# Context and token transfers issued first, and VectorE in place of ScalarE for the turned exponentials of three attentions

## The chip, the cores and the metric

The kernel runs on one core of one Trainium2 chip. The metric is the device time of one launch in microseconds (us), the median of several runs. Engines are written as the profile writes them: PE is TensorE (PEld its weight loads), ACT is ScalarE, DVE is VectorE, POOL is GpSimd, SP is SyncE, which here only issues transfers.

## What is computed

Four blocks run one after the other on x (16 x 128 tokens, 256 channels) with a context ctx of the same shape, all in fp32:

```python
x = _L0_xattn_ref(ctx, x, ...)   # 16 heads of 16: tokens attend to context and tokens (256 keys); MLP with gelu
x = _L1_xattn_ref(x, ctx, ...)   # 32 query heads on 8 key heads of 8: attend to the context (128 keys); layer norm
x = _L2_xattn_ref(x, ctx, ...)   # recurrent block: token shift, low-rank mixes, decays, scan over 128 tokens, channel mix
x = _L3_xattn_ref(x, ctx, ...)   # 16 heads of 16: attend to the normalised context (128 keys); gated residual
```

The three attentions (of blocks 0, 1 and 3) are softmax(q k + mask) v.

## The kernel before

The 16 sequences are worked off in eight pairs. The work on a pair is cut into four parts, entry (transposes of x and ctx, q, k and v of block 0, k and v of block 1), front (blocks 0 and 1), back (block 2 and the queries of block 3) and final (attention 3 and the output). The parts of neighbouring pairs are interleaved in phases: `start` has the entry of pair 0, `first` the front of pair 0 and the entry of pair 1, `second` front, back and entry of three steps, five `steady` passes have all four parts, and `closing`, `last` and `end` run the pipeline empty. `last` holds the back of the last pair and attention 3 of the pair before; `end` holds attention 3 of the last pair alone.

**The order of work is written out by hand.** Four texts, PE_ORDER, ACT_ORDER, DVE_ORDER and POOL_ORDER, list the steps of each engine in the order in which it runs them, `@` giving the phase. Every engine works its list off in order, and each step waits on counting semaphores for what it needs. So what stands in front of a step on its own engine sets when it can begin.

An attention job n is a chain of five steps. `scores` (PE, L719, four jobs at a time into the four banks psS), `mask` (DVE, L1213: mask and negated maximum, into one of four buffers S), `exps` (ACT, L1029: exponentials and their sum, into one of two buffers E), `turn` (PE, L730: four 128x128 transposes into one of three ring banks of PSUM) followed by the copy of that bank into one of four buffers ET, and `weigh` (PE, L764 or L772: product with the values into psO). Attentions 0 and 1 have 16 jobs for a pair, attention 3 has 8. Which engine copies the turned exponentials is fixed by the table EMPTIES: ACT (L1016) for attentions 0 and 3, DVE (L1229) for attention 1. Every other product of PE goes through the same three ring banks, and a bank is written again only when the product three places earlier in PE's list has been copied out.

Names that come up later: `xT`, `cT` transposes of tokens and context; `q0`, `k0l`, `k0c`, `v0c`, `v0l`, `k1`, `v1` the entry's products; `aT` the normalised context; `norm`/`apply` the layer norms (DVE, with a root on POOL); `sum` the product with the inverse sums; `o1` the output of attention 1; `xaT`, `shift1`, `t` the head of block 2 (transpose L669, token shift, low-rank product L887); `vr0` to `vr7` its scans (DVE L1425, L1432), each followed by a product on POOL (L1569); `bonus` (L1412) and `g2` (L1407) two more steps of it on DVE; `yT`, `ynT` its group norm (L935, L669).

Before the lists there is a setup. SP issues W0 (q, k and v weights of block 0 in one transfer), the column constants colt, all seven bias rows rowt and the one-number gate, all on the semaphore s_w, and then context, tokens and mask of pair 0 and the other weights. PE, ACT, DVE and POOL each wait for all four transfers on s_w (64), and PE and POOL for DVE's constants too, before their first step:

```python
            sp.dma_start(W0t[:, 0:qkv], wl0[:, 0:qkv]).then_inc(s_w, 16)
            ...
            pe.wait_ge(s_setup_d, 4)
            pe.wait_ge(s_w, WEIGHTS_IN)
```

## Time and profile before

| | |
|---|---|
| median of three runs | 1126.52 us (1123.29 to 1128.92) |
| the profiled execution, its own time | 1128.1 us |
| its span | 1126.1 us |
| PE busy | 980.3 us, 87% |
| DVE busy | 806.4 us, 72% |
| ACT busy | 739.1 us, 66% |
| POOL busy | 256.7 us, 23% |
| mean granted clock of PE | 0.955 |

A busy share is an average over stages with different limits, so the kernel is read stage by stage. A row of the trace gives the start of a piece and its length, the engine and the line, and in brackets how long the engine had been idle before it and what ended that. The time of an execution is some 2 us more than its span.

### The profile page before, as it was taken

To read this page: it belongs to the slowest core of one execution; us is meant where nothing else is said; L and a number is where in the kernel's file an instruction comes from. 1 tells how busy PE (TensorE), PEld (TensorE's weight loads), DVE (VectorE), ACT (ScalarE), POOL (GpSimd) and SP (SyncE) were. 2 spreads that over 40 slices of the span, in tenths; PEclk is the share of its full clock that TensorE was granted. 3 is DMA by queue.
4 is the path that set the end of the run, shared out by engine and by line. 5 is a ranking of instruction groups with operands and counts; after the bars stand their busy time and mean duration, and the time that the engine had idled before them with its cause. 6 is when DMAs were issued, how large, how long until landed. Compare 5 with 4: busy or idle time off the path is not lost.

```text
span 1126.1 us, 23973 instructions
## 1 busy us (share of the span) xinstructions
PE 980.3 (87%) x7776; PEld 699.8 (62%) x7776; DVE 806.4 (72%) x3113; ACT 739.1 (66%) x2675; POOL 256.7 (23%) x349
## 2 busy tenths in 40 slices
PE   5779898998999899998999899998999899888356
PEld 4456566765766577665767577665766577556144
DVE  3408758886878776977878777987878776966623
ACT  1828853887658973788658983887658973881116
POOL 3102304031320413032321413031311413120300
PEclk9889999999999999999999999999999999989576
DMA  9100000000010000000010001000010000000000
GB/s 303 41 1 17 6 1 24 2 8 2 2 33 8 2 2 20 16 8 1 2 33 8 2 2 28 7 8 2 1 33 8 2 2 10 2 3 10 0 1 10
DMA packets 18091, 18.90 MB, mean 17 GB/s; under 512 B 7216, under 2 KB 16432, under 8 KB 17712
## 3 DMA queue, kind: packets, MB, share of 16 engines
q1 hardware_dynamic: 17968, 17.37, 5.1%
q8 instruction: 64, 1.05, 0.4%
q14 instruction: 59, 0.48, 0.1%
HBM read 15.27 MB, written 2.10 MB: 15 GB/s over the span
## 4 chain that ended last, share of the span: by engine, by line
PE 60%; DVE 14%; ACT 10%; issue 6%; POOL 2%; POOLq 0%; DVEq 0%; ACTq 0%
PE ring L678 16%; PE ring L688 15%; PE ring L730 9%; PE psS L719 5%; ACT E L1029 5%; DVE S L1213 3%; PE psO L764 2%; PE psO L772 2%; PE ring L897 2%; PE ring L669 2%; PE psO L805 2%; PE ring L887 1%; DVE slot L1389 1%; PE psS L788 1%; DVE SS L1432 1%
## 5 line engine op out<-in xcount | busy, mean ns | idle before, releaser
L1029 ACT ACTIVATE E<-S,nmax 128x128 f32<-128x128 f32 (+1 forms) x1024 | 423.7, 419 | 32.4 <-PE ring L730 21.3
L1213 DVE CUSTOM_DVE_ANT_0 S<-psS,mb 128x128 f32<-128x128 f32 (+1 forms) x1024 | 263.0, 319 | 39.8 <-ACT E L1029 17.2
L678 PE MATMUL ring<-slot,w_l 128*128 128x256 f32 x992 | 243.9, 393 | 16.5 <-ACT slot L990 12.3
L730 PE MATMUL ring<-ident,E 128*128 128x128 f32 x1280 | 202.3, 289 | 29.5 <-ACT E L1029 25.3
L678 PEld LDWEIGHTS ring<-slot,w_l 128*128 128x128 f32 x992 | 185.5, 195 | 54.8 <-ACT slot L990 14.6
L730 PEld LDWEIGHTS ring<-ident,E 128*128 128x128 f32 x1280 | 144.9, 145 | 101.8 <-ACT E L1029 63.0
L1029 ACT ACTIVATION_READ_ACCUMULATOR E<-S,nmax 128x1 f32 x1024 | 195.6, 191 | 0.0
L688 PE MATMUL ring<-w_l,slot 128*128 128x256 f32 (+1 forms) x640 | 155.1, 387 | 12.1 <-DVE slot L1453 4.7
L688 PEld LDWEIGHTS ring<-w_l,slot 128*128 128x128 f32 x640 | 116.3, 196 | 42.5 <-issue 8.8
L1016 ACT ACTIVATE ET<-ring 128x512 f32<-128x512 f32 x192 | 106.9, 587 | 17.2 <-PE ring L730 17.1
L719 PE MATMUL psS<-keys,slot 32*128 32x512 f32 (+1 forms) x768 | 97.3, 580 | 21.4 <-ACT ET L1016 12.8
L1432 DVE TENSOR_TENSOR_SCAN SS<-wP,kv 128x258 f32<-128x258 f32 x128 | 98.3, 809 | 9.7 <-POOL Z L1569 7.7
L990 ACT ACTIVATE slot<-ring 128x512 f32<-128x512 f32 x72 | 42.6, 594 | 81.1 <-PE ring L669 56.5
L1229 DVE COPY ET<-ring 128x512 f32<-128x512 f32 x128 | 84.1, 685 | 16.1 <-PE ring L730 16.1
L669 PE MATMUL ring<-ident,slot 128*128 128x128 f32 x384 | 62.9, 292 | 32.6 <-DMA slot<-in_x 12.8
L1213 DVE DVE_READ_ACCUMULATOR2_ANT nmax<- 128x1 f32 x1024 | 85.3, 83 | 0.0
L1569 POOL TENSOR_TENSOR Z<-SS,slot 128x512 f32<-128x512 f32 x64 | 77.1, 1204 | 35.7 <-DVE SS L1432 19.0
L1541 POOL TENSOR_TENSOR keys<-k0T,in 128x512 f32<-128x512 f32 x32 | 33.1, 1044 | 219.1 <-PE psS L719 212.7
L669 PEld LDWEIGHTS ring<-ident,slot 128*128 128x128 f32 x384 | 44.2, 146 | 55.5 <-issue 19.5
L1117 ACT ACTIVATE slot<-ring 128x512 f32<-128x512 f32 x8 | 4.8, 598 | 101.0 <-PE ring L935 101.0
L764 PE MATMUL psO<-ET,V 128*32 128x128 f32 x1536 | 64.8, 291 | 4.0 <-ACT ET L1016 3.3
L719 PEld LDWEIGHTS psS<-keys,slot 32*128 32x128 f32 x768 | 34.5, 187 | 38.6 <-ACT ET L1016 14.1
(120 smaller groups left out, 1131.7 us busy)
## 6 DMA issues: line engine op xcount, KB each, us to landing
slot<-in_ctx SPq DMA_DIRECT2D x8, 256.0 KB, 2.8
slot<-in_x SPq DMA_DIRECT2D x8, 256.0 KB, 2.8
w_l<-in_wl SPq DMA_DIRECT2D x1, 2048.0 KB, 10.7
out<-slot SPq DMA_DIRECT2D x8, 256.0 KB, 2.1
w_l<-in_wl SPq DMA_DIRECT2D x2, 768.0 KB, 6.6
w_l<-in_wl SPq DMA_DIRECT2D x1, 1152.0 KB, 8.5
m0i<-in_m SPq DMA_DIRECT2D x8, 128.0 KB, 3.1
mb<-in_m SPq DMA_DIRECT2D x8, 128.0 KB, 2.5
```

The costliest lines, as they stand in the source:

```text
L669: m = pe.transpose(b[:, c, a * P:(a + 1) * P], src[:, a, c * P:(c + 1) * P], ident[:, :])
L678: m = pe.matmul(b[:, a, :], w[:, k, m0 + a * P:m0 + (a + 1) * P], src[:, k, :], start=(k == 0), stop=(k == kt - 1))
L688: m = pe.matmul(b[:, bb, 0:n], src[:, k, bb * P:(bb + 1) * P], w[:, k, :], start=(k == 0), stop=(k == kt - 1))
L719: ins = pe.matmul(psS[m % QUAD][:, x * w:(x + 1) * w], queries, keys[rows, group % RING_K, x * w:(x + 1) * w], start=True, stop=True)
L730: m = pe.transpose(b[:, k, :], E[:, g % RING_E, k * P:(k + 1) * P], ident[:, :])
L764: m = pe.matmul(psO[32 * c:32 * c + 32, t, bb * P:(bb + 1) * P], v[:, window(8 * t + 4 * half + c, half, 16)], e, start=(half == 0 and sbl ...
L1016: act.activation(ET[:, g % 4, :, :], bank(phase, i, turned).rearrange("p a (h s) -> p (a h) s", h=2), ACT.Copy).then_inc(sems["emptied_A"], 1)
L1029: ins = act.activation(E[:, g % RING_E, h * w:(h + 1) * w], S[:, g % RING_S, h * w:(h + 1) * w], ACT.Exp, bias=nmax[:, g % 4, h:h + 1], sc ...
L1213: ins = dve.tensor_tensor_reduce(S[:, g % RING_S, h * w:(h + 1) * w], psS[g % QUAD][:, h * w:(h + 1) * w], bias[:, bb, :], -1.0, HUGE, ALU ...
L1229: dve.tensor_copy(ET[:, g % 4, :, :], bank(phase, i, turned).rearrange("p a (h s) -> p (a h) s", h=2))\
L1432: ins = dve.tensor_tensor_scan(SS[:, u % 2, a, :, :].rearrange("p b t -> p (b t)"), wP[:, ct, :, :].rearrange("p b t -> p (b t)"), kv[:, u ...
L1569: pool.tensor_tensor(Z[:, v % RING_Z, :, :].rearrange("p a (b t) -> p a b t", b=PAIR), SS[:, v % 2, :, :, 0:P], r, ALU.mult).then_inc(sems ...
```

## The change

1. SP issues context, tokens and mask of pair 0 first. The q, k and v weights of block 0 come as three transfers with a semaphore each, the two value-bias rows (128 partitions each) on their own, then W1, the gate and, after a wait for the v weights, the other five rows. Only colt still counts on s_w.
2. PE waits at the start for the identity only, and then at each product for its own weights. ACT and DVE wait for colt. POOL waits for the two head masks. DVE builds its other constants later, at its step `cols`, and the spread matrix is one copy of 256 columns in place of eight. The gate's tanh moves behind `aT`.
3. The table TURNED gives three attentions' turned exponentials to DVE: attention 0 of pair 0 (16 copies, phase `first`), attention 3 in `last` (8) and in `end` (8).
4. The four order texts are written anew, from `start` to `end`. Waits for score and output banks are found from the list of stages; they ask for the same events as before.

```diff
+TURNED = {("first", 0): "D", ("end", 3): "D", ("last", 3): "D"}
+def emptier(phase, name):
+    engines = TURNED.get((phase, name[1])) if name[0] == "turn" else None
+    return engines[name[2] % len(engines)] if engines else EMPTIES[name]
...
-            sp.dma_start(W0t[:, 0:qkv], wl0[:, 0:qkv]).then_inc(s_w, 16)
-            sp.dma_start(colt[:, :, :], cols).then_inc(s_w, 16)
-            sp.dma_start(rowt[:, :, :], rows.partition_broadcast(P)).then_inc(s_w, 16)
-            sp.dma_start(gate_t[:, 0:1], gate.partition_broadcast(P)).then_inc(s_w, 16)
...
             program("start", None)
+            sp.dma_start(W0t[:, 0:CT * C], wl0[:, 0:CT * C]).then_inc(s_wq, 16)
+            sp.dma_start(W0t[:, CT * C:2 * CT * C], wl0[:, CT * C:2 * CT * C]).then_inc(s_wk, 16)
+            sp.dma_start(colt[:, :, :], cols).then_inc(s_w, 16)
+            sp.dma_start(W0t[:, 2 * CT * C:qkv], wl0[:, 2 * CT * C:qkv]).then_inc(s_wv, 16)
+            for n in (ROWS.index("v0_b"), ROWS.index("v1_b")):
+                sp.dma_start(rowt[:, n:n + 1, :], rows[:, n:n + 1, :].partition_broadcast(P)).then_inc(s_row, 16)
             sp.dma_start(W1t[:, :], wl1).then_inc(s_w1, 16)
+            sp.dma_start(gate_t[:, 0:1], gate.partition_broadcast(P)).then_inc(s_gate, 16)
+            sp.wait_ge(s_wv, 16)
+            sp.dma_start(rowt[:, 1:len(ROWS) - 1, :], rows[:, 1:len(ROWS) - 1, :].partition_broadcast(P)).then_inc(s_rows, 16)
...
-            pe.wait_ge(s_setup_d, 4)
-            pe.wait_ge(s_w, WEIGHTS_IN)
+            pe.wait_ge(s_const, 2)
...
-            act.wait_ge(s_w, WEIGHTS_IN)
             act.wait_ge(s_const, 3)
-            act.activation(gate_t[:, 1:2], gate_t[:, 0:1], ACT.Tanh).then_inc(s_setup, 1)
+            act.wait_ge(s_w, 16)
...
-                    elif step[0] == "turn" and EMPTIES[step] == "D":
+                    elif step[0] == "turn" and emptier(phase, step) == "D":
                         copy_turned(*step[1:])
...
-            pool.wait_ge(s_w, WEIGHTS_IN)
-            pool.wait_ge(s_setup_d, 4)
+            ins.then_inc(s_zeros, 1)
+            pool.wait_ge(s_in32, 1)
```

Of the rewritten lists, three places show what moves.

ACT, from its first instruction (L984, before, is the gate's tanh; L990 and L1025 the copy of xT; L1001 and L1036 the keys; L1016 the copies of turned exponentials). Before:

```order
L984 ACT_TABLE_LOAD [waits s_const]
L984 ACTIVATE gate_t<-gate_t 128x1 [waits weights_in]
L990 ACTIVATE slot<-ring 128x512 [waits s_product]
L1001 ACTIVATE k0T<-ring,colt 128x2x128 [waits s_product]
L1001 ACTIVATE k0T<-ring,colt 128x2x128
```

and with the change:

```order
L1025 ACT_TABLE_LOAD [waits s_product,weights_in]
L1025 ACTIVATE slot<-ring 128x512 [waits s_const]
L1036 ACTIVATE k0T<-ring,colt 128x2x128 [waits s_product]
L1036 ACTIVATE k0T<-ring,colt 128x2x128
L1064 ACTIVATE E,esum<-S,nmax 128x256 [waits s_masked]
```

The load of the function table stood in front of the waits for the transfers; now it stands behind the wait for xT's product and for colt, directly in front of xT's copy. The first exponentials follow the keys at once, with `k1` behind them.

PE, the end of attention 0 in the second steady pass (L719 and L757 are `scores`, L730 and L768 `turn`, L764 and L792 `weigh`, L887 and L923 `t`; the 128x256 scores are those of attention 3). Before:

```order
L669 MATMUL ring<-ident,slot 128x128 [waits s_emptied_A,s_n2]
L730 MATMUL ring<-ident,E 128x128 [waits s_emptied_A,s_exps]
L719 MATMUL psS<-keys,slot 128x256 [waits s_keys,s_masked,s_emptied_A]
L719 MATMUL psS<-keys,slot 128x256 x7
L764 MATMUL psO<-ET,V 32x128 [waits s_emptied_A]
L887 MATMUL ring<-slot,w_l 128x256 [waits s_emptied_A,s_xxx]
L887 MATMUL ring<-slot,w_l 32x256 x2
```

and with the change:

```order
L693 MATMUL ring<-ident,slot 128x128 [waits s_emptied_A,s_n2]
L757 MATMUL psS<-keys,slot 128x512 [waits s_keys,s_masked]
L792 MATMUL psO<-ET,V 32x128 [waits s_emptied_A]
L768 MATMUL ring<-ident,E 128x128 [waits s_emptied_A,s_exps]
L923 MATMUL ring<-slot,w_l 128x256 [waits s_emptied_A,s_xxx]
L923 MATMUL ring<-slot,w_l 32x256 x2
L757 MATMUL psS<-keys,slot 128x256 [waits s_keys,s_masked,s_emptied_A]
```

(rows that only repeat are left out). The transpose for block 2 comes in front of the last scores of attention 0, and the first scores of attention 3 come behind `t` instead of two turns and one weigh in front of it.

DVE, the end of the program (L1213 and L1241 are masks, L1257 the copies of turned exponentials; four masks make a job). Before:

```order
L1213 ISA S,nmax<-psS,mb 128x128 [waits s_exps,s_scores]
L1237 RECIPROCAL einv<-esum 128x2x16 [waits s_exps]
L1239 COPY slot<-einv 128x512 [waits s_inverse3]
L1246 TENSOR_TENSOR slot<-psO,slot 128x512 [waits s_pv,s_emptied_A]
L1488 SCALAR_TENSOR_TENSOR slot<-ring,gate_t,slot 128x512 [waits s_out_done,s_x4,s_product]
```

and with the change:

```order
L1257 COPY ET<-ring 128x512 [waits s_pv,s_product]
L1241 ISA S,nmax<-psS,mb 128x128 [waits s_exps,s_scores]
L1257 COPY ET<-ring 128x512 [waits s_pv,s_product] x7
L1278 RECIPROCAL einv<-esum 128x2x16 [waits s_exps]
L1280 COPY slot<-einv 128x512 [waits s_inverse3]
L1287 TENSOR_TENSOR slot<-psO,slot 128x512 [waits s_pv,s_emptied_A]
L1541 SCALAR_TENSOR_TENSOR slot<-ring,gate_t,slot 128x512 [waits s_out_done,s_setup,s_x4,s_product]
```

One copy stands between the fourth and the fifth job's masks, and seven behind the last mask.

## Rows read from the trace of the kernel before

**Rows 1.** The page: busy times; PE in 40 slices; one transfer, issue to landing.

```profile
PE 980.3 (87%) x7776; PEld 699.8 (62%) x7776; DVE 806.4 (72%) x3113; ACT 739.1 (66%) x2675; POOL 256.7 (23%) x349
...
PE   5779898998999899998999899998999899888356
...
slot<-in_ctx SPq DMA_DIRECT2D x8, 256.0 KB, 2.8
```

**Rows 2.** Busy times by stretch; 263.30 to 389.80 is one steady pass.

```profile
core 0: us, PE busy (x) PEld busy (x) DVE busy (x) ACT busy (x) POOL busy (x), PEclk, DMA share, GB/s
25.47:56.59 31.12, 23.16 (x238) 13.89 (x237) 15.73 (x75) 25.48 (x83) 5.09 (x6) 0.89 0.20 57
263.30:389.80 126.50, 117.97 (x973) 84.80 (x973) 99.13 (x387) 91.46 (x333) 31.73 (x41) 1.00 0.04 10
504.00:522.00 18.00, 14.76 (x168) 8.98 (x164) 13.41 (x70) 16.88 (x59) 8.11 (x10) 1.00 0.01 1
```

**Rows 3.** DMA of the first 14 us, in 40 slices of 0.35 us.

```profile
GB/s 0 0 0 0 53 193 35 246 298 439 404 387 408 415 432 410 410 451 307 62 0 0 12 220 284 328 366 405 451 430 440 418 380 395 300 411 193 111 492 263
```

**Rows 4.** Timeline of the start: start us, us, engine, line, operation.

```profile
1.17 0.42 SPq L578 DMA_DIRECT2D colt<-in_cols  x1
...
5.64 1.28 ACT L984 ACT_TABLE_LOAD   x1 [5.64 <-POOL eps_g L1506]
...
10.24 0.75 DVE L1177 BATCH_NORM_STATS2 bst<-slot 128x6 f32<-128x256 f32 x2 [2.03 <-DMA slot<-in_ctx]
...
12.13 0.60 ACT L990 ACTIVATE slot<-ring 128x512 f32<-128x512 f32 x1 [3.30 <-PE ring L669]
...
12.78 7.61 PE L678 MATMUL ring<-slot,w_l 128*128 128x256 f32 x24
...
23.68 1.03 PE L678 MATMUL ring<-slot,w_l 128*128 128x256 f32 x4
...
25.47 1.14 PE L719 MATMUL psS<-keys,slot 32*128 32x512 f32 x8
```

**Rows 5.** Groups by line in attention 0 of pair 0, 25.4 to 56.6 us.

```profile
L1029 ACT ACTIVATE E<-S,nmax 128x256 f32<-128x256 f32 x32 | 15.8, 503 | 0.8 <-PE ring L730 0.8
...
L1016 ACT ACTIVATE ET<-ring 128x512 f32<-128x512 f32 x16 | 8.8, 588 | 1.7 <-PE ring L730 1.7
```

**Rows 6.** Timeline of the phase `last`, DVE.

```profile
989.90 1.29 DVE L1229 COPY ET<-ring 128x512 f32<-128x512 f32 x2 [2.20 <-PE ring L730]
...
1007.49 0.75 DVE L1177 BATCH_NORM_STATS2 bst<-slot 128x6 f32<-128x256 f32 x2 [2.80 <-POOL slot L1633]
...
1013.81 0.88 DVE L1380 SCALAR_TENSOR_TENSOR slot<-slot,colt,shifted 128x256 f32<-128x256 f32 x2
```

**Rows 7.** Timeline of the phase `last`, PE, from 985 us.

```profile
1017.98 2.01 PE L887 MATMUL ring<-slot,w_l 128*128 128x256 f32 x8
```

**Rows 8.** The chain that ended last, from 1022 us.

```profile
1041.04 0.58 DVE slot L1412
1041.62 0.59 DVE slot L1407
...
1106.69 0.48 ACT ET L1016
```

**Rows 9.** Groups by line in the phase `end`, 1096 to 1119 us.

```profile
L1029 ACT ACTIVATE E<-S,nmax 128x128 f32<-128x128 f32 x32 | 12.4, 393 | 2.4 <-DVE nmax L1213 2.4
```

**Rows 10.** Waits of PE in five passes, 263 to 894 us.

```profile
PE psS L719 <- ACT ET L1016: 10.7, 5, 2.1
PE ring L678 <- ACT slot L990: 8.5, 5, 1.7
```

**Rows 11.** Timeline, PE at attention 3's first scores.

```profile
513.70 1.15 PE L719 MATMUL psS<-keys,slot 32*128 32x256 f32 x16 [2.14 <-ACT ET L1016]
```

**Rows 12.** Timeline, PE between `yT` and `ynT`.

```profile
444.99 1.05 PE L935 MATMUL ring<-centre,slot 128*128 128x128 f32 x8
...
450.86 1.39 PE L669 MATMUL ring<-ident,slot 128*128 128x128 f32 x8 [0.25 <-DMA slot<-in_ctx]
```

More of the change, by code:

```diff
@@ L23 @@
 DECAY = 64
-WEIGHTS_IN = 4 * 16
 BIG = 1e30
@@ L131 @@
+k3 @closing weigh1.12 weigh1.13 weigh1.14 @last turn3.0 @closing sum1 weigh1.15 @last scores3.4 turn3.1 @closing o1
+@last turn3.2 turn3.3 weigh3.1 turn3.4 weigh3.3 turn3.5 turn3.6 turn3.7 weigh3.5 weigh3.7 xaT v3 sum3 t o3 mw mk mv d1
+d2 k2 mr mg v2 r2 vp0 bonus vp1 gather3 g2 gather7 yT ynT o2 xcT fr fk fv x4T q3 @end scores3.0 turn3.0 scores3.4
+turn3.1 turn3.2 turn3.3 weigh3.1 turn3.4 weigh3.3 turn3.5 weigh3.5 turn3.6 turn3.7 weigh3.7 sum3 o3
 """
 ACT_ORDER = """
[L134 removed]
@@ L180 @@
+x4T exps1.12 exps1.13 q3 exps1.14 exps1.15 @last exps3.0 exps3.1 k3 @closing sum1 @last exps3.2 exps3.3 exps3.4
+exps3.5 exps3.6 exps3.7 xaT sum3 t d1 d2 decay k2 r2 g2 yT yn ynT xcT fr fk x4T q3 @end exps3.0 exps3.1 exps3.2
+exps3.3 exps3.4 exps3.5 exps3.6 exps3.7 sum3
 """
 DVE_ORDER = """
-@first norm3 mask0 @start cT @first apply3 cols @start q0 v0c v0l v1 @first mask0.0 mask0.1 mask0.2 mask0.3 mask0.4
-mask0.5 mask0.6 mask0.7 mask0.8 @second norm3 @first mask0.9 mask0.10 cT mask0.11 @second apply3 @first mask0.12
@@ L240 @@
-vr1 bonus g2 vr2 vr3 vr4 vr5 vr6 vr7 yT yn y2 o2 norm4 apply4 shift0 fv @end mask3.0 mask3.1 mask3.2 mask3.3 mask3.4
-mask3.5 mask3.6 mask3.7 inv3 sum3 o3
+@first mask0 @start cT @first cols @start q0 @first norm3 apply3 @start v0c v0l @first mask0.0 mask0.1 @start v1
+@first mask0.2 mask0.3 mask0.4 turn0.0 turn0.1 mask0.5 turn0.2 turn0.3 mask0.6 mask0.7 turn0.4 turn0.5 mask0.8 mask0.9
+mask0.10 mask0.11 turn0.6 turn0.7 @second norm3 @first turn0.8 turn0.9 mask0.12 mask0.13 turn0.10 mask0.14 cT turn0.11
@@ L242 @@
+@last turn3.7 @closing apply2 @last inv3 shift1 v3 sum3 o3 mw mk mv mr mg v2 ruk vr0 vr1 vr2 vr3 vr4 vr5 vr6 vr7 bonus
+g2 yT yn y2 o2 norm4 apply4 shift0 fv @end mask3.0 mask3.1 mask3.2 mask3.3 turn3.0 mask3.4 mask3.5 mask3.6 mask3.7
+turn3.1 turn3.2 turn3.3 turn3.4 turn3.5 turn3.6 turn3.7 inv3 sum3 o3
 """
 POOL_ORDER = """
-@first norm3 sum0 scores0.0 scores0.4 scores0.8 scores0.12 @second norm3 @first scores1.0 hn x1T @second scores0.0
-scores0.4 scores0.8 @first norm1 @second scores0.12 @first apply1 @second sum0 @first norm2 @second scores1.0 hn vr0
@@ L1317, in program @@
                     elif step == "cols":
+                        if phase == "first":
+                            constants()
                         dve.wait_ge(leaves("cT"), earlier_left("cT"))
```

509 lines of the change are left out of this document (269 added, 240 removed).

## The prediction

> **What bounds the kernel now.** I read the page first, then the busy times by stretch, then the start and the two last phases in the timeline and in the chain of waits. The page gives PE 980 us of a span of 1126, and the 40 slices show where the other 146 are: the first three and the last five slices stand at 3 to 8 tenths, those between at 8 and 9 [rows 1]. In a steady pass of 126.5 us PE is busy 118.0, DVE 99.1, ACT 91.5 [rows 2], so a pass cannot shrink by more than 8.5 us, whatever the order. At both ends PE waits for a chain, and a microsecond taken out of the chain is one off the time.
>
> Three such chains are touched. The first is the start: nothing runs on PE until tokens and context are in at 10 to 11 us, and xT's copy (12.13) and the first product of weights (12.78) follow [rows 4]. The second is attention 0 of pair 0, from its first scores at 25.47 [rows 4] to o0 at 56.59: of these 31.1 us ACT is busy 25.5, DVE 15.7, PE 23.2 [rows 2]. The third is the last 110 us: block 2 of the last pair and the attentions around it.
>
> **The change part by part, against the profiled execution (1128.1 us).**
>
> *Leading transfers.* Before, DMA ran in one stretch from 1.4 to about 7 us and then stood still for more than a microsecond before context came [rows 3]; the sum of that stretch is 4950 GB/s times 0.35 us, 1.7 MB, which is W0's 768, the rows' 896 and colt's 27 KB. With the change colt is the sixth transfer, with 256 + 256 + 128 + 256 + 256 + 27 = 1179 KB up to and with it. The same slices reach 1179 KB at 5.3 us. SP issues one transfer in some 0.5 us, and colt, issued at 1.17 before [rows 4], would be issued near 3.3; it lands near 6.0. Context, tokens and their transposes on PE are through by then, but ACT and DVE wait for colt. DVE's cT copy is ready early. ACT has one thing more: its table load (1.28 us) was over at 6.9, under the transfers [rows 4]; now it stands behind the wait for xT's product and colt. So 6.0 + 1.28 + 0.60 for xT's copy [rows 4] puts the first product of weights at 7.95, against 12.78: **-4.8**. The bounds: tokens at their old rate of 256 KB in 0.77 us (context ends DVE's wait at 10.24, tokens PE's at 11.0) would bring colt at 7.9, a gain of 2.9; a hidden table load gives 6.1. I take the slices' rate, since it is that of the very same transfers.
>
> The products q0 to v0l keep their lengths. k1, which ran in front of the first scores comes behind them; its four matmuls take 1.03 us from 23.68 [rows 4], some 0.17 of it beside v1's: **-0.9**. v1 needs W1, 704 KB further down the queue, near 9 us; PE is there near 19. The value bias rows and POOL's zeros (memsets of under 5 us) are covered in the same way, and the wait that SP now makes for the v weights only delays rows that POOL uses near 40 us. DVE's constants, one microsecond, fall into its wait for q0's product. All this costs nothing; if the cover fell away, it would be that microsecond.
>
> *Attention 0 of pair 0.* ACT loses 16 copies, 8.8 us busy [rows 5], and has some 16 left. DVE gains 16. Two copies back to back take 1.29 us there [rows 6], so 0.64 each, 10.3 in all. DVE's 15.7 [rows 2] lose 0.7 for a layer norm's second half that now comes later, which makes 25.3; with 1.3 us from scores to the first mask's start, 0.9 for the last weigh and 1 us of waits between, the stretch takes 28.5 us in place of 31.1: **-2.5**. The bounds: 0, if DVE meets as much idle time as ACT has now (5.6), and -3.7, with no waits between. A mask and its copy now share an engine, and the exponentials wait for masks, so I stay away from the lower end.
> The Trainium skill (Perfetto Trace Analysis, Optimizing Scalar/DVE Operations) speaks against this move: it charges DVE 125 ns and ScalarE 51 ns of overhead for PSUM operands. The copies of this trace have that sign, 0.64 against 0.48 us back to back; by the rule's difference 32 copies cost 2.4 us of engine time more, which counts only while DVE is the bound.
>
> *The phase `last`.* Block 2 starts with `t` at 1017.98 [rows 7], though its input (DVE L1380) was done at 1014.69 [rows 6]: a weigh, a transpose and v3 stood in front. Now weigh comes before, v3 fills the wait, and only the transpose for `sum3` stays. DVE gets eight copies between its norms, 5.1 us; the norm waited 2.80 us for POOL there [rows 6], which takes four of them, and ACT's exponentials end 8 x 0.48, some 4 us, earlier. I set the input 1.5 us later: `t` at 16.3 in place of 18.2, **-1.9**. Bounds: 0 and -3.3. Further on `bonus` and `g2` (0.58 and 0.59 us on the chain [rows 8]) leave the place between scans 1 and 2 for the wait of three microseconds behind scan 7: **-1.2**, or 0 if yT then waits for them.
>
> *The phase `end`.* The chain goes through ACT: 32 exponentials, 12.4 us [rows 9], and eight copies at 0.48 [rows 8]. Without the copies it is 3.8 us shorter; the last copy takes 0.1 more on DVE, and a copy that sits behind the last four masks holds a ring bank for some 0.4: **-3.2**. Bounds -1.5 and -3.8.
>
> *The middle.* The orders of all passes are new, with the same instructions. In five passes PE loses 10.7 us in front of attention 3's first scores and 8.5 in front of q1 [rows 10]; the first is a wait of 2.14 us a pass [rows 11]. The scores now stand behind `t`, which should take most of that away, but PE runs into ACT there: in 18 us around this place ACT is busy 16.9 [rows 2], so what PE does not wait for at the scores it will wait for at the turns. The second lies between yT and ynT (444.99 to 451.6) [rows 12], a chain over ACT, DVE and a table load; cT has left the place in front of ynT in most passes, 0.6 us of cover less, and in two passes x1T comes before yT. k1 (0.9) moves into the stretch in which PE waits for ACT. I net this to **-2**; bounds -13 (all of the scores' waits, in six passes) and +7.
>
> Sum: -4.8 - 0.9 - 2.5 - 1.9 - 1.2 - 3.2 - 2.0 = -16.5, so 1111.6 against the profiled execution's 1128.1. The median of the runs is 1.6 lower than that execution, which makes **1110**.
>
> **Rivals.**
>
> *The passes shrink too.* If the wait of 2.14 us is gone in six passes and comes back nowhere, the middle gives 12.8 and not 2: 1099. For it: PE has 8.5 us idle in a pass. Against: ACT's 16.9 of 18.
>
> *VectorE takes ACT's place as bound.* Then neither attention gets shorter and block 2 starts no earlier: 2.5, 3.2 and 1.9 are lost, 1117.6. For it: DVE would be at 26 of 31 us, more than ACT is now. Against: most of ACT's idle 5.6 us lie before its first and behind its last job.
>
> *The leading transfers don't overlap.* A context load by itself takes 2.8 us from issue to landing [rows 1]. If each of the six paid that in turn, colt would land near 17 and the first product come at 19, a loss of 6.2 in place of the 4.8: 1121. Against it stands the unbroken stretch of 1.7 MB [rows 3].
> The Trainium skill (DMA: Bandwidth & Descriptors, Anatomy of one DMA) gives a DMA 2.0 us fixed plus its bytes over 436 GB/s; in series the six would take 14.7 us by it and the time would come near 1119, overlapped it agrees with the slices.
>
> *ScalarE runs dry, and the kernel gets slower.* Attention 3's first scores now come behind a weigh, a turn or two and `t`, together 0.6 + 2 x 0.6 + 1.9 = 3.7 us of PE work. If the four masks ahead don't bridge that, ACT, the bound of that stretch, stands idle 3.7 us in each of six passes: +22.2, with the other terms' -14.5 a result near 1134. It decides from 3.4 us a pass on, where 20 us eat the gain and 0.5% more; at half force it is no change. For it: ACT busy 16.9 of 18. Against: the scores now wait 2.14 us anyway, so they come only 1.6 later, and S holds four jobs, about 4 us of ACT's work.
>
> **How the numbers follow.** A measurement of this kernel tells 0.5% from no change, 5.6 us. I give the forecast 0.56 (its own range 1103 to 1117), shrinking passes 0.16, VectorE as bound 0.14, transfers in turn 0.04, ScalarE dry 0.05 and the same at half force 0.05. Below 1120.9, faster, lie the first two and most of the third: 0.85. Within 0.5%: 0.10. Slower: 0.05. The range 1098 to 1121 takes in most of the second case, the third and half of the fourth, and leaves out the last two and the fringes.
>
> **What would show it.** The first product of weights near 8 us, ACT's table load directly in front of xT's copy; first scores near 20; o0 near 48; DVE over 85% busy between. Steady passes of 125 to 127 us. In `end`, 23 us from the first scores of attention 3 to the last copies become under 20. The forecast is wrong if a pass differs by more than a microsecond from 126, if colt lands behind 8 us, or if DVE's copies keep attention 0 at 31.

## The result, and the profile after

| | us | ratio to before |
|---|---|---|
| before, four runs beside after | 1127.72 (1123.29 to 1135.02) | |
| after, four runs | 1145.71 (1142.40 to 1151.56) | 1.0159, 95% interval 1.009 to 1.0227 |
| predicted | 1110, range 1098 to 1121 | |

The kernel became 18 us slower, and the prediction was wrong in sign. The profiled execution of after took 1151.56 us, its span is 1148.7; it is the slowest of the four, 5.9 us above their median, and every stage below is read from it. Before's profiled execution is 0.4 us above its median.

The page of the kernel after, busy times and two rows of slices:

```profile
PE 991.8 (86%) x7776; PEld 702.3 (61%) x7776; DVE 838.3 (73%) x3139; ACT 724.2 (63%) x2643; POOL 256.2 (22%) x349
...
PE   6689897999989899988989899898999899888456
...
PEclk9999999999999999998999999999999999998576
```

The first slices of PE are fuller than before [rows 1]: the start gained. The last ones are nearly as they were. Where the time went, stage by stage (the borders are the starts of `t` on TensorE in the phases second to last):

```profile
core 0: us, PE busy (x) PEld busy (x) DVE busy (x) ACT busy (x) POOL busy (x), PEclk, DMA share, GB/s
0.00:139.49 139.49, 107.19 (x828) 74.72 (x829) 81.05 (x351) 77.55 (x289) 31.02 (x48) 0.96 0.23 74
139.49:261.31 121.82, 108.43 (x845) 76.78 (x846) 91.28 (x316) 74.70 (x260) 29.66 (x39) 0.99 0.03 8
261.31:393.44 132.13, 118.97 (x979) 85.48 (x977) 104.20 (x396) 93.21 (x341) 31.94 (x41) 0.99 0.03 10
393.44:523.42 129.98, 118.64 (x985) 85.13 (x985) 103.79 (x392) 92.45 (x338) 33.15 (x43) 1.00 0.04 10
523.42:656.60 133.18, 122.83 (x972) 87.50 (x972) 102.42 (x388) 90.99 (x332) 28.74 (x40) 0.96 0.03 10
656.60:786.75 130.15, 118.41 (x972) 84.97 (x972) 100.44 (x389) 92.69 (x339) 31.93 (x43) 1.00 0.03 10
786.75:915.03 128.28, 119.42 (x932) 84.12 (x933) 100.85 (x373) 87.94 (x321) 31.24 (x41) 0.97 0.03 10
915.03:1038.70 123.67, 111.69 (x927) 79.93 (x925) 98.24 (x400) 87.92 (x341) 26.67 (x39) 0.96 0.02 4
1038.70:1148.70 110.00, 66.19 (x344) 43.66 (x344) 56.01 (x144) 26.76 (x89) 11.86 (x18) 0.69 0.02 5
```

Before, the same nine stages took 142.8, 120.3, 126.6, 126.8, 125.6, 126.7, 125.9, 123.4 and 108.1 us. So the start won 3.3, the second phase lost 1.5, the five steady passes lost 5.6, 3.2, 7.6, 3.4 and 2.4 (22.2 together), closing 0.3, and the stretch from the last `t` to the end 1.9. Nearly all of the loss lies where the diff changes nothing but orders.

The same five passes as one stretch, first before, then after:

```profile
263.10:894.60 631.50, 588.68 (x4862) 424.87 (x4861) 498.22 (x1935) 458.36 (x1668) 157.60 (x205) 1.00 0.04 10
```

```profile
261.31:915.03 653.72, 598.28 (x4838) 427.20 (x4837) 511.71 (x1934) 457.28 (x1665) 157.01 (x206) 0.98 0.03 10
```

PE's idle time went from 42.8 to 55.4 us, its busy time from 588.7 to 598.3 for the same matmuls. Of the latter 8.5 us is the clock: in slices of 2 us before shows one stretch at half speed in these passes, after six, each of which loses 1.7 us.

What PE waits for in them, after (us in total, times, longest), to be held against [rows 10]:

```profile
PE ring L693 <- DVE slot L1500: 8.2, 5, 2.9
PE ring L768 <- ACT E L1064: 7.5, 17, 1.1
PE ring L693 <- DVE slot L1217: 4.4, 3, 2.8
PE ring L702 <- ACT slot L1025: 3.5, 4, 1.2
PE psO L830 <- POOL Z L1623: 3.3, 6, 0.8
PE ring L693 <- DVE slot L1280: 2.8, 3, 1.8
```

The wait of 10.7 us in front of attention 3's first scores is gone, as predicted, and that in front of `q1` (L702) fell from 8.5 to 3.5. But transposes (L693) now wait 16.3 us in all, against 2.3 before: 8.2 at `ynT` for the group norm's end (L1500), 3.7 at `xaT` and 0.7 at `xcT` for layer norms (L1217), 2.5 at `sum3` for the inverse sums (L1280). And the gathers (L830) wait 3.3 us for POOL's Z, 2.5 of them at `gather7`; before they waited for nothing in these passes.

The start of after:

```profile
3.17 0.43 SPq L641 DMA_DIRECT2D colt<-in_cols  x1
...
3.62 1.94 PE L693 MATMUL ring<-ident,slot 128*128 128x128 f32 x8 [3.62 <-DMA slot<-in_ctx]
...
8.06 1.28 ACT L1025 ACT_TABLE_LOAD   x1 [8.06 <-DMA colt<-in_cols]
...
9.35 0.60 ACT L1025 ACTIVATE slot<-ring 128x512 f32<-128x512 f32 x1
...
10.00 1.22 PE L702 MATMUL ring<-slot,w_l 128*128 128x256 f32 x2 [4.45 <-ACT slot L1025]
```

Colt is issued where I said (3.17 for 3.3) but lands at 8.0 in place of 6.0; behind it come the table load and xT's copy exactly as worked out. The DMA of the first 14 us, in slices of 0.35 us as in [rows 3]:

```profile
GB/s 0 0 0 0 0 32 190 375 354 386 287 181 123 108 164 109 205 293 329 313 356 287 325 344 351 481 418 418 382 341 223 220 234 202 181 240 331 322 100 506
```

Between 3.9 and 6 us the queue moves 108 to 205 GB/s, where before it moved about 400. It reaches 1179 KB at 6.9 us; in [rows 3] that was 5.3. The first product of weights starts at 10.00 for 12.78 [rows 4].

Attention 0 of pair 0, from its first scores to `o0`:

```profile
22.61:50.56 27.95, 21.16 (x240) 13.11 (x240) 24.17 (x89) 18.34 (x69) 5.58 (x5) 1.00 0.35 117
```

27.95 us against 31.12 [rows 2], VectorE busy 86%.

### The profile page after: what moved, and what is told of

Same layout as the page of the kernel before. It is cut to its first block, busy times and chain, and to the rows that moved or that the text cites. A ratio compares the mean times of both kernels' runs of the same rounds, so it can differ in the third digit from the quotient of the medians.

```text
span 1148.7 us, 23987 instructions
## 1 busy us (share of the span) xinstructions
PE 991.8 (86%) x7776; PEld 702.3 (61%) x7776; DVE 838.3 (73%) x3139; ACT 724.2 (63%) x2643; POOL 256.2 (22%) x349
## 4 chain that ended last, share of the span: by engine, by line
PE 32%; DVE 14%; ACT 10%; issue 7%; POOL 3%; DVEq 0%; POOLq 0%; ACTq 0%
PE ring L702 7%; PE ring L712 6%; ACT E L1064 6%; PE ring L768 5%; DVE S L1241 3%; PE psS L757 2%; DVE SS L1484 2%; POOL Z L1623 2%; PE ring L693 2%; PE psO L792 2%; PE psO L800 1%; PE ring L933 1%; PE ring L923 1%; PE psO L830 1%; DVE kv L1477 1%
## 5 line engine op out<-in xcount | busy, mean ns | idle before, releaser
L1064 ACT ACTIVATE E<-S,nmax 128x128 f32<-128x128 f32 (+1 forms) x1024 | 423.9, 418 | 61.8 <-PE ring L768 33.6
L1241 DVE CUSTOM_DVE_ANT_0 S<-psS,mb 128x128 f32<-128x128 f32 (+1 forms) x1024 | 262.0, 318 | 31.0 <-PE psS L757 17.6
L702 PE MATMUL ring<-slot,w_l 128*128 128x256 f32 x992 | 245.7, 395 | 14.3 <-ACT slot L1025 10.0
L768 PE MATMUL ring<-ident,E 128*128 128x128 f32 x1280 | 204.6, 289 | 35.3 <-ACT E L1064 23.9
L702 PEld LDWEIGHTS ring<-slot,w_l 128*128 128x128 f32 x992 | 186.3, 196 | 58.0 <-ACT slot L1025 13.8
L768 PEld LDWEIGHTS ring<-ident,E 128*128 128x128 f32 x1280 | 143.8, 145 | 111.5 <-ACT E L1064 63.0
L712 PE MATMUL ring<-w_l,slot 128*128 128x256 f32 (+1 forms) x640 | 154.9, 387 | 11.5 <-DVE slot L1505 3.2
L1257 DVE COPY ET<-ring 128x512 f32<-128x512 f32 x160 | 106.3, 683 | 23.0 <-PE ring L768 22.6
L1484 DVE TENSOR_TENSOR_SCAN SS<-wP,kv 128x258 f32<-128x258 f32 x128 | 107.6, 881 | 6.5 <-POOL Z L1623 4.5
L1051 ACT ACTIVATE ET<-ring 128x512 f32<-128x512 f32 x160 | 90.0, 589 | 33.4 <-PE ring L768 33.3
L1025 ACT ACTIVATE slot<-ring 128x512 f32<-128x512 f32 x72 | 42.4, 593 | 102.5 <-PE ring L693 88.3
L757 PE MATMUL psS<-keys,slot 32*128 32x512 f32 (+1 forms) x768 | 95.7, 578 | 10.2 <-DVE nmax L1241 6.3
L693 PE MATMUL ring<-ident,slot 128*128 128x128 f32 x384 | 63.7, 295 | 39.9 <-DVE slot L1500 12.4
L1241 DVE DVE_READ_ACCUMULATOR2_ANT nmax<- 128x1 f32 x1024 | 84.2, 82 | 0.0
L693 PEld LDWEIGHTS ring<-ident,slot 128*128 128x128 f32 x384 | 45.0, 148 | 61.7 <-DVE slot L1500 14.5
L1595 POOL TENSOR_TENSOR keys<-k0T,in 128x512 f32<-128x512 f32 x32 | 33.3, 1052 | 206.5 <-PE psS L757 204.3
L792 PE MATMUL psO<-ET,V 128*32 128x128 f32 x1536 | 63.3, 289 | 6.0 <-DVE ET L1257 4.0
L792 PEld LDWEIGHTS psO<-ET,V 128*32 128x32 f32 x1536 | 38.4, 113 | 35.0 <-issue 18.7
L712 PE MATMUL ring<-w_l,hT 128*128 128x256 f32 x256 | 57.4, 382 | 0.9 <-ACT hT L1036 0.9
```

The costliest lines, as they stand in the source:

```text
L693: m = pe.transpose(b[:, c, a * P:(a + 1) * P], src[:, a, c * P:(c + 1) * P], ident[:, :])
L702: m = pe.matmul(b[:, a, :], w[:, k, m0 + a * P:m0 + (a + 1) * P], src[:, k, :], start=(k == 0), stop=(k == kt - 1))
L712: m = pe.matmul(b[:, bb, 0:n], src[:, k, bb * P:(bb + 1) * P], w[:, k, :], start=(k == 0), stop=(k == kt - 1))
L757: ins = pe.matmul(psS[m % QUAD][:, x * w:(x + 1) * w], queries, keys[rows, group % RING_K, x * w:(x + 1) * w], start=True, stop=True)
L768: m = pe.transpose(b[:, k, :], E[:, g % RING_E, k * P:(k + 1) * P], ident[:, :])
L792: m = pe.matmul(psO[32 * c:32 * c + 32, t, bb * P:(bb + 1) * P], v[:, window(8 * t + 4 * half + c, half, 16)], e, start=(half == 0 and sbl ...
```

## The experiments

Verdicts are ratios to the kernel before on the same chip; before's median lies between 1128.2 and 1132.8 us on them. One execution of each kernel is profiled. The places of steps are read from TensorE's timeline and given in us behind the `t` that opens the pass.

**1. Which part of the change loses: start, middle or ends.**

`a_setup`: the changed setup, no order changed, `TURNED = {}`.

> The changed kernel's leading transfers and constants, with every order and every copy as before. Theory (the losses lie in the orders of the passes, the leading transfers gain what the trace of after shows): the first product of weights starts at 10.0 us in place of 12.78, first scores near 22.7, and the time is 2.8 us under before, 1125. Rival (the gain at the start is eaten by the time pair 0 reaches the second phase, because something later bounds it): first scores near 22.7, but t of the second phase within 1 us of before's 142.8, the time 1127 to 1128.

`b_start_first`: with the orders of start and first and VectorE's copies there.

```diff
-TURNED = {("first", 0): "D", ("end", 3): "D", ("last", 3): "D"}
+TURNED = {("first", 0): "D"}
```

> As the last one, with the changed kernel's order of the start and first phases and VectorE's copies in attention 0 of pair 0 as well. Theory: o0 of pair 0 starts 6.0 us earlier than before (50.6 for 56.6) as in after, and since the later phases have the old orders nothing takes it back: 1122. Rival (the 2.3 us that after lost between m2 of pair 0 and t of the second phase belong to the first phase's order): 1124.5. Third (the copies on VectorE gain nothing without the new passes): 1125, as the last one.

`c_old_middle`: in all four order texts the steps of the phases second to closing stand as in before, the rest as changed.

> The changed kernel with the four orders of before in the phases second to closing; start, first, last and end stay as changed. Theory (the new order of the passes is the whole loss): steady passes of 126 to 127 us again, no wait for POOL's Z in front of the gathers, and 1127.7 - 5.6 (start and first) - 1 (last) = 1121. Rival A (last and end lose 2 us with the copies on VectorE, as after's 110.0 from the last t to the end against 108.1 say): 1124. Rival B (the passes are long because of the lead that the start gives, or by the clock, not by their order): 1140 or more.

| | median us | ratio (95%) | first scores | o0 | t of second | five passes |
|---|---|---|---|---|---|---|
| before | | | 25.5 | 56.6 | 142.8 | 631.5 |
| a_setup | 1124.6 | 0.9961 (0.9936 to 0.9987) | 22.2 | 52.4 | 139.0 | 631.0 |
| b_start_first | 1129.9 | 1.0015 (0.9995 to 1.0036) | 21.5 | 51.0 | 142.4 | 630.7 |
| c_old_middle | 1126.4 | 0.9983 (0.996 to 1.0005) | 23.2 | 51.2 | 141.7 | 632.1 |
| after | 1145.7 | 1.0159 (1.009 to 1.0227) | 22.6 | 50.6 | 139.5 | 653.7 |

The third run settles it: with the old orders in the middle the passes are 126 us again, under the same lead, the same copies and the same setup. Its passes 1 and 2:

```profile
388.50:514.90 126.40, 117.20 (x974) 84.54 (x973) 99.82 (x387) 91.72 (x336) 30.89 (x41) 1.00 0.04 10
514.90:640.50 125.60, 117.87 (x975) 85.06 (x973) 99.16 (x387) 91.52 (x336) 32.22 (x41) 1.00 0.04 10
```

The setup alone is worth about 4 us. The second run, 5 us above the slowest of its three expectations, shows something I had not priced: the new order of the first phase behind `o0` gives the start's gain back. `o0` comes 5.6 us earlier than before, `t` of the second phase only 0.4 (3.3 in after, with the new second phase behind it). From `o0` to that `t` it takes 91.4 us, before 86.2. The third run shares this loss (90.5 us), so it ends at 1126.4, nearer to rival A's 1124 than to the 1121 of the theory, though its passes are as the theory said.

**2. Three guesses at one culprit.** POOL's order, and attention 3's first scores (my rival that ended on the slow side), each put back in after (`x_pool_only`, `after_s30_first`); the scores also moved in before (`before_s30_late`).

`x_pool_only`:

> The changed kernel with POOL's order alone as before in the phases second to closing. Theory P (POOL's order makes the gathers wait for Z, 7.0 us in the middle against 0.5 before, and the layer norms come late, 4.7 us): those waits go, 1134 to 1140. Rival (POOL only follows VectorE's scans, which come later by VectorE's own order): within 3 us of after's 1145.7, with the wait in front of the gathers still over 4 us.

`after_s30_first`:

> The changed kernel with scores3.0 in front of t in steady0, steady1 and closing, the three phases in which it stands behind t. ScalarE theory (attention 3's scores come too late and ACT runs dry): ACT's idle time in front of its exponentials falls from 61.8 us towards 32.4, the time by 8 us or more, under 1138. Chain theory: the first scan comes 1 us earlier behind t, but TensorE waits some 2 us in front of the scores again, time within 3 us of 1145.7.

```diff
 steady1 of after, TensorE
-turn0.11 turn0.12 t scores3.0 turn0.13
+turn0.11 turn0.12 scores3.0 t turn0.13
```

`before_s30_late`:

> The kernel before with scores3.0 directly behind t in steady0 to steady4, everything else as it was. ScalarE theory: ACT stands idle up to 3.7 us in each of five passes, up to 1147. Chain theory: the wait of 2.1 us in front of scores3.0 moves or goes, t comes up to 3 us earlier in the pass, the scans come 1 us later behind t, so time 1120 to 1129.

```diff
 steady1 of before, TensorE
-turn0.10 scores3.0 turn0.11 weigh0.9 turn0.12 t turn0.13
+turn0.10 turn0.11 weigh0.9 turn0.12 t scores3.0 turn0.13
```

Measured, in the same order: 1154.3 us, 1.0223 (1.019 to 1.0256); 1152.9 us, 1.0209 (1.0175 to 1.0243); 1129.8 us, 1.001 (0.9987 to 1.0033). Neither of the first two is better than after, and the intervals do not tell whether they are worse; so POOL's order alone is not the culprit. In before the scores may stand on either side of `t`: from the second phase to closing PE's wait in front of them falls from 12.8 to 2.1 us, and PE now waits 9.9 us in front of attention 0's turns for ScalarE's copies (0.6 before). The rival on ScalarE falls, in both kernels. In after_s30_first ACT's idle time in front of its exponentials is 60.5 us, against 61.8 in after:

```profile
L1061 ACT ACTIVATE E<-S,nmax 128x128 f32<-128x128 f32 (+1 forms) x1024 | 424.0, 418 | 60.5 <-PE ring L765 31.8 <-DVE nmax L1238 27.7
```

**3. Delaying the chain in the kernel before.** What after's passes have in common is the stretch from `t` to `ynT`:

| | steady0 | 1 | 2 | 3 | 4 |
|---|---|---|---|---|---|
| before: vp0 / gather3 / ynT | 25.0 / 42.5 / 61.8 | 26.3 / 40.9 / 61.9 | 25.0 / 42.5 / 61.8 | 26.8 / 42.0 / 61.3 | 24.8 / 42.3 / 61.6 |
| after: vp0 / gather3 / ynT | 24.9 / 48.7 / 66.9 | 29.5 / 46.2 / 63.8 | 33.3 / 47.8 / 67.3 | 29.1 / 46.2 / 65.0 | 29.7 / 47.6 / 64.7 |
| ynT later by | 5.1 | 1.9 | 5.5 | 3.7 | 3.1 |
| pass longer by | 5.6 | 3.2 | 7.6 | 3.4 | 2.4 |

What comes behind `ynT` takes the same time in both kernels within some 2 us. The chain is: `t`, mixes, `k2` to `g2`, `vp0` (TensorE spreads the values), scans 0 to 3 on VectorE with Z on POOL, `vp1`, `sum3` (the end of attention 3, whose sum frees the bank that `gather3` writes), `gather3`, scans 4 to 7, `gather7`, yT, the group norm, `ynT`. Three edits delay one link each in before (the cut shows TensorE's list; before_vp0_late also moves VectorE's first scans, before_a3_late ScalarE's copy of `sum3`, each with its product):

```diff
 steady0 of before, TensorE: before_vp0_late
-vp0 bonus weigh3.1 turn3.4 weigh3.3 turn3.5 nT k3
+bonus weigh3.1 turn3.4 weigh3.3 turn3.5 nT k3 vp0
 before_vp1_late
-u1 vp1 weigh3.7 sum3 u2 u3 gather3
+u1 weigh3.7 sum3 u2 u3 vp1 gather3
 before_a3_late
-u1 vp1 weigh3.7 sum3 u2 u3 gather3
+u1 vp1 u2 u3 weigh3.7 sum3 gather3
```

`before_vp0_late`:

> The kernel before with one thing moved in the phases steady0 to closing: TensorE's vp0 (which spreads the values for the first four scans) behind k3 and nT, and VectorE's vr0 (and vr1) behind the copy of nT, which is where the changed kernel has them in its worst pass. Nothing is added. Chain theory (after t a pass lasts as long as the chain t, mixes, vp0, eight scans, gather7, yT, ynT; in after the first scan comes 6.9, 3.2, 8.3, 1.9 and 4.9 us later behind t than before, and those passes are 5.6, 3.2, 7.6, 3.4 and 2.4 us longer): first scan some 5 us later, passes of 130 to 132 us, time 1129 + 5 x 4.5 = 1151. Bound theory (TensorE is busy 93 of 100 and only does the same work in another order): passes of 126 to 127, time within 3 us of 1129.

`before_vp1_late`:

> The kernel before with vp1 behind u3 in steady0 to closing, nothing else. Theory L: two to three u products, 3.8 to 5 us, come in front of it, the last scan ends 3 us later, and ynT and the end of the pass with it: six passes of 129 to 130, time 1128 + 18 = 1146. Rival (only the first scan decides, the second half has slack because m2's 7 us on TensorE hide it): within 3 us of 1128.

`before_a3_late`:

> The kernel before with weigh3.7 and sum3 behind u3 in steady0, steady2, steady3, steady4 and closing, nothing else. Theory S: u2 and u3 (3.8 us) and more come in front of sum3, gather3 starts near 45 to 46 in place of 42.5, ynT and the pass come 3 to 4 us later in each of the five, time 1129 + 16 = 1145. Rival (attention 3 has slack, only the value spreads matter): within 3 us of 1129.

| | median us | ratio (95%) | steady0, 2, 4: ynT later by | pass longer by |
|---|---|---|---|---|
| before_vp0_late | 1172.8 | 1.0387 (1.0356 to 1.0419) | 7.9, 7.6, 7.9 | 9.3, 7.6, 8.8 |
| before_vp1_late | 1143.4 | 1.0137 (1.0107 to 1.0167) | 2.9, 4.5, 2.9 | 2.9, 5.7, 2.9 |
| before_a3_late | 1138.0 | 1.0054 (1.0032 to 1.0076) | 1.7, 2.3, 2.1 | 3.4, 2.4, 2.2 |

All three slow the kernel and add no work, so these three links have no slack in the order of before, and in them a late `ynT` goes with a longer pass nearly one for one. The distance from `t` is not a loss by itself: in before_s30_late `ynT` comes 1.1 to 2.0 us later behind `t`, but `t` comes earlier, and the time stays. before_vp1_late came near its 1146. The first cost twice what I expected. TensorE takes its steps in order, so a late link also stops what is queued behind it:

```profile
PE psS L785 <- DVE kv L1422: 18.0, 4, 4.7
```

Here PE waits in front of `vp1` for VectorE's fourth product, 18.0 us from steady0 to closing, none there before. The last edit did a third of what I expected, since `gather3` followed `sum3` by 2.1 us in place of 4.

**4. Bringing the chain forward in the kernel after.** If lateness of a link is the cause, moving it forward should repair after.

`after_vp0_early`:

> The changed kernel with vp0 brought forward in steady0, steady2, steady3, steady4 and closing to directly behind the last of r2, g2, k2, v2, d2, and vr0 in front of nT and bonus. Chain theory: vp0 comes 4.7 us earlier in steady2, 1.8 and 1.2 in steady3 and steady4, up to 2 in closing, nothing in steady0 but nT's wait; the passes give back about that, 1145.7 - 7 = 1139. Rival (the passes are long for other reasons, the waits only show up there): within 2 us of 1145.7.

`after_vp1_early`:

> The changed kernel with vp1, which spreads the values for the last four scans, directly behind u1 in steady0 to closing, where the kernel before mostly has it; in after it stands behind u2, sum3 and turns, and comes at 39.9 to 45.8 us behind t against 36.7 to 39.0. Theory L (the pass follows the end of the last scan, which is 53.5 to 56.5 us behind t in after against 49.1 to 50.4): that end comes 2 to 4 us earlier, passes near 128, time 1146 - 12 = 1134. Rival (the scans before it are late too, and TensorE now waits in front of vp1 for VectorE's fourth product, with u2 and u3 queued behind): waits in front of vp1 of 1 us or more a pass, time 1144 or more.

`after_vp0_vp1`:

> The changed kernel with vp0 and vr0 brought forward as in after_vp0_early and vp1 directly behind u1 as in after_vp1_early. Alone the first did nothing (1145.9), the second cost 24 us, because TensorE waited in front of vp1 (18.6 us in six passes) for VectorE's fourth product, which was late. Chain theory (both have to be early): with the first scans at 29 to 30 us behind t the wait at vp1 shrinks under 1.5 us a pass, the last scan ends at 51 to 53, passes 128 to 129, time 1138. Rival (VectorE's own order holds the scans: nT, bonus, inv3, sum3 between them wait for TensorE's later products): the wait at vp1 stays over 2 us a pass and the time over 1150.

`after_chain_old` (the last one is `after_vp0_vp1`):

> As the last one, and VectorE takes vr0 to vr7, bonus, nT, inv3, sum3 and m2 in the order of before (in all but steady1), with TensorE's bonus directly behind vp0 in steady2, steady3, steady4 and closing, and k3 behind nT in steady2. Chain theory: the scans follow one another as before, the last ends at 50 to 52 us behind t, ynT comes at 62 to 63, the five steady passes fall to 126 to 128, time 1146 - 15 = 1131. Rival (the loss isn't in this chain but in the turns and transposes after it, which keep the new order): passes stay at 129 or more, time 1140 or more.

`after_a3_early`:

> The changed kernel with the end of attention 3 (turn3.6, turn3.7, the last weighs, sum3 on TensorE; the turn copies and sum3 on ScalarE) directly behind u0, and vp1 behind u1, in steady0 to steady3 and closing. New theory S: sum3 decides. VectorE's sum for attention 3 stands in its queue in front of the last scans and frees the bank that gather3 writes, and gather3 frees what POOL's Z of the last four needs; in every profile so far ynT starts 17 to 19 us behind gather3. In after sum3 starts 40.4 to 44.9 us behind t, before 35.0 to 38.9. Here it should start near 38 to 40, gather3 at 43 to 45, ynT 3 us earlier than in after, time 1146 - 13 = 1133. Rival (the chain is held by the first scans, as the runs with vp0 and vp1 left possible): a wait in front of vp1 takes what sum3 gives, time 1143 or more.

`after_all_early`:

> The changed kernel with all three brought forward: vp0 and vr0 as in after_vp0_early, vp1 behind u1, and the end of attention 3 behind u0. Theory S with the chain: no wait left in front of vp1, sum3 at 38 to 40, last scan at 50 to 52, passes 127 to 128, time 1146 - 18 = 1128. Rival (what the new order lengthened is elsewhere): 1140 or more.

```diff
 steady2 of after, TensorE: after_all_early
-g2 k3 weigh3.1 nT bonus turn3.4 vp0 turn3.5 u0 u1 weigh3.3 turn3.6 turn3.7 u2 weigh3.5 weigh3.7 sum3 u3 vp1 gather3
+g2 vp0 k3 weigh3.1 nT bonus turn3.4 turn3.5 u0 weigh3.3 turn3.6 turn3.7 weigh3.5 weigh3.7 sum3 u1 vp1 u2 u3 gather3
```

| | median us | ratio (95%) | wait in front of vp1, second to closing | five passes |
|---|---|---|---|---|
| after | 1145.7 | 1.0159 (1.009 to 1.0227) | 1.0 | 653.7 |
| after_vp0_early | 1145.9 | 1.0154 (1.0118 to 1.019) | 1.0 | 651.1 |
| after_vp1_early | 1169.5 | 1.0352 (1.032 to 1.0383) | 18.6 | 673.8 |
| after_vp0_vp1 | 1162.0 | 1.0301 (1.028 to 1.0321) | 11.6 | 664.1 |
| after_chain_old | 1167.4 | 1.0344 (1.0327 to 1.036) | 7.1 | 666.6 |
| after_a3_early | 1156.0 | 1.0199 (1.0164 to 1.0234) | 1.0 | 661.1 |
| after_all_early | 1156.1 | 1.0202 (1.0177 to 1.0228) | 1.1 | 658.2 |

None repairs it, and what the chain theory expected, 1128 to 1139, is wrong for all six. (The 2.6 us that the passes of after_vp0_early seem to save are no gain: after's profile is its slowest execution, and the medians are the same.) Each move makes another wait. In `after_vp0_vp1` VectorE stands in front of its sum for attention 3 with scans behind it, and POOL's Z waits for `gather3`. VectorE, then POOL:

```profile
702.20 1.50 DVE L1481 TENSOR_TENSOR_SCAN SS<-wP,kv 128x258 f32<-128x258 f32 x2
709.90 0.69 DVE L1284 TENSOR_TENSOR slot<-psO,slot 128x512 f32<-128x512 f32 x1 [6.20 <-ACT slot L1022]
```

```profile
703.78 0.21 POOL L1630 TENSOR_TENSOR kv<-s,wP 128x4 f32<-128x4 f32 x1 [1.21 <-DVE SS L1481]
711.90 1.59 POOL L1620 TENSOR_TENSOR Z<-SS,slot 128x512 f32<-128x512 f32 x1 [7.91 <-PE psO L827]
```

That pointed to the end of attention 3. Brought forward, it makes PE wait 8.9 us in front of its weighs from steady0 to last (1.0 in after), for copies that come no sooner, and `gather3` stays at 46 to 56. So it is shown that the order of the passes is the loss, and that it appears as a late `ynT` and more half-speed stretches. That the chain from `t` to `ynT` is the cause, and not one more place where the loss shows, is argued from the delays in before and not shown: no move of one link, nor of three, repaired after. Of the four texts only POOL's was put back alone; TensorE's, ScalarE's and VectorE's were not. Which step a repair would have to start from stays open; only all four old texts together did it.

**5. The start, and a kernel that beats both.**

```diff
+            sp.dma_start(colt[:, :, :], cols).then_inc(s_w, 16)
             program("start", None)
             sp.dma_start(W0t[:, 0:CT * C], wl0[:, 0:CT * C]).then_inc(s_wq, 16)
             sp.dma_start(W0t[:, CT * C:2 * CT * C], wl0[:, CT * C:2 * CT * C]).then_inc(s_wk, 16)
-            sp.dma_start(colt[:, :, :], cols).then_inc(s_w, 16)
```

`colt_first`:

> As a_setup (changed setup, old orders and copies, 1124.6), with colt's transfer issued ahead of context and tokens. In after context and tokens are transposed from 3.62 us, but ACT waits for colt until 8.02, then loads its table. Theory (colt is the last thing missing at the start): colt lands near 4 us, the table load ends near 5.5, xT's copy near 6.2 and the first product of weights starts when wq is there, near 6.5 in place of 9.9: 1121. Rival (wq lands with the others at 8 to 9 us): first product at 9 or later, 1124.

1126.1 us, 0.9979 (0.9961 to 0.9997), where 1121 or 1124 was expected.

```profile
5.94 1.28 ACT L1023 ACT_TABLE_LOAD   x1 [5.94 <-PE ring L691]
7.24 0.60 ACT L1023 ACTIVATE slot<-ring 128x512 f32<-128x512 f32 x1
...
8.27 1.62 PE L700 MATMUL ring<-slot,w_l 128*128 128x256 f32 x3 [1.58 <-DMA w_l<-in_wl]
```

Colt no longer holds ACT, and now the product waits for the weights of q0, which land at 8.2. 1.6 us are won there over a_setup, and lost by `o0` (53.4 against 52.4), for a reason not looked into. The time doesn't show them.

`best_mix` has before's orders behind `o0` of pair 0, the changed setup with colt first, the changed order and VectorE's copies up to that `o0`, and those of the phase end.

> The kernel before in its orders from the first phase's o0 on, with the changed setup and colt's transfer first, the changed order and VectorE's copies up to o0 of pair 0, and VectorE's copies and the changed order in the phase end. If the parts add: 3.5 for the setup, 3.4 for colt, 2 for attention 0 of pair 0 (27.9 us from first scores to o0 in place of 30), 2 for end (20.5 in place of 22.4): 1128 - 11 = 1117. If what is won at the start is lost again before the second phase, as in b_start_first: 1124.

1121.2 us (1119.7 to 1125.7), 0.9934 (0.9911 to 0.9958): 0.7% faster than before, 2% than after, and 4 us above the sum of the parts, 1117. First scores at 21.1, `o0` 49.0, `t` of the second phase 135.7 for 142.8. That is 7 us, where the parts' sum said 9; the end gave nothing. From `o0` to `t` it takes 86.7 us in before's order, 91.4 in b_start_first in the changed one: that order is what gave the start's gain back there.

## Why the prediction was wrong, step by step

*Leading transfers, -4.8.* Mechanism right, size wrong: -2.8 at the first product, and in a_setup, where nothing else changes, -3.8 at the second `t`. What failed in this term is "it lands near 6.0", and with it "that of the very same transfers". I read off the old slices [rows 3] when the bytes in front of colt would be through, 5.3 us, and set the landing 0.7 us behind that. The new sequence doesn't run at the old rate: it falls to 108 to 205 GB/s between 3.9 and 6 us and has moved those bytes at 6.9. Colt was complete 1.1 us later, at 8.02, just beyond my upper bound of 7.9 and the 8 us that I had named as a sign of being wrong. Which transfer slows the queue no run separates. The Trainium skill (DMA: Bandwidth & Descriptors, Anatomy of one DMA) says of DMAs issued by GpSimd that the fixed cost is mostly the wait for the confirmation that the last byte has landed; here SyncE issues them, and no run splits the 4.85 us from colt's issue to its landing.

*k1, -0.9.* Not seen: from the first product of weights to the first scores 12.61 us, against 12.69, though k1 has gone from between. Profiles that share an order there differ by more than the term (11.4 to 12.7 us in before's, 11.5 to 13.0 in after's), so it is neither shown nor refuted.

*Attention 0 of pair 0, -2.5.* Right. The stretch is 27.95 us where I had 28.5, VectorE is busy 24.2 where I had 25.3; with ACT's copies and the new setup it takes 30.2 (a_setup), so the copies and the order that goes with them win 2.3 (0.7 by the profile of b_start_first, where the stretch is 29.5). The rival in which VectorE takes ACT's place as bound did not happen. But I took a microsecond won at `o0` for one off the time, without pricing the new order between there and the next `t`: b_start_first shows that it takes back all but 0.4.

*last, -1.9 and -1.2.* From attention 3's first scores to `t` 26.6 us in place of 27.7, but that is no gain shown: the other profiles with before's order there take 25.2 to 27.8, those with after's 26.2 to 29.4. `bonus` and `g2` left their place between scans 1 and 2, and from `vp0` to `vp1` the chain takes 9.2 us in place of 9.95, in every profile: -0.7 of the -1.2. The rest is lost because the next pair of scans, now begun earlier, begins while POOL's Z is under way and takes 1.93 us in place of 1.28, before and then after:

```profile
1042.85 1.28 DVE L1432 TENSOR_TENSOR_SCAN SS<-wP,kv 128x258 f32<-128x258 f32 x2
```

```profile
1064.44 1.93 DVE L1484 TENSOR_TENSOR_SCAN SS<-wP,kv 128x258 f32<-128x258 f32 x2
```

From `t` to `vp0` it is 19.2 in place of 16.9: there the clock loses 3.4 us in after and nothing in before. Before's own order takes 16.9, 18.6 or 19.9 us there, with 0, 1.7 or 3.4 us lost by the clock, and after's 19.2 to 19.5 in all ten profiles: the difference is the clock's, and whether the new order brings the low clock on stays open.

*end, -3.2.* Nothing: 23.3 us from the first scores of attention 3 to `o3`, 23.0 before. The copies did leave ACT (13.3 us busy for 17.1). What ate the gain is TensorE's clock, in after and, for comparison, in c_old_middle, with the same orders and copies:

```profile
1118.43:1141.69 23.26, 15.76 (x132) 10.59 (x133) 13.65 (x75) 13.34 (x65) 0.00 (x0) 0.63 0.00 1
```

```profile
1098.74:1119.27 20.53, 12.42 (x132) 8.28 (x132) 13.66 (x75) 13.23 (x65) 0.00 (x0) 0.83 0.00 1
```

At a granted clock of 0.83 the stretch is 20.5 us, at 0.63 it is 23.3, and in best_mix at 0.57 it is 24.0. With ACT's copies it was 22.4 at 0.77, 23.0 at 0.70 and 24.1 at 0.64. At like clocks VectorE's copies win about one (23.3 against 24.1 at 0.63 and 0.64); which clock a run gets there decides more than they do. Over all profiles the stretch takes 23.0 us on average with ACT's copies (8 of them) and 22.6 with VectorE's (11).

*The middle, -2, bounds -13 and +7.* This is the step that failed, and it alone turned the sign: +22.2 in five passes of the profiled execution, three times the upper bound. I read the waits of before as a list [rows 10] and asked of each whether the new order takes it away. It does (10.7 us gone, 5.0 of 8.5 gone). I did not ask what the moved steps stand in front of now. I noted that `cT` leaves the place in front of `ynT`, "0.6 us of cover less"; the waits for the group norm around `q1` and `ynT` went from 8.8 to 11.7. And I never followed the chain `t` to `ynT` through both orders, though the order texts show k3, nT and bonus in front of `vp0`, and u2, o3 and turns in front of `vp1` and `gather3`. "The same instructions" was taken for "the same length". The line of the prediction that would have shown it wrong, a pass that differs by more than a microsecond from 126, is what came, in all five.

*The slow rival* had the place wrong (ScalarE at attention 3's scores), though its number, 1134, was on the right side. That its term is 22.2 us, as the measured loss is, is chance. Its chance of 0.05, and 0.05 at half force, was far too low for a change that rewrites all four orders of passes in which TensorE idles only 8.5 us of 126.

## What to carry to other kernels

In a pipeline with an order written by hand for each engine, an order is good as a whole: price a new one by following its longest chain through all engines, link by link, and not by the waits that it removes. In passes in which TensorE was 93% busy, three of the four single moves tried in a matched order cost 0.5 to 3.9%, and the fourth nothing, so adding no work does not make a move free. Change the ends and the middle apart: here the start could be kept without the middle, and only the start was worth having.
